# Identity products in TensorE's waits, and expert weights read from HBM tile by tile, in a perceiver layer with a mixture of experts

## What is computed

```
x = x + cross_attention(context, context, layernorm(x))      # 16 heads of 8
x = x + latent_attention(layernorm(x))                       # 8 heads, compressed keys and values
x = x + experts(layernorm(x))

def experts(x):                                              # 8 experts, 2 for each row, I = 352
    logits = x @ w_router.T;  probs = softmax(logits)
    topw, topi = top_k(probs, 2);  topw = topw / sum(topw)
    gate = silu(einsum('th,eih->eti', x, w_gate))
    up   = einsum('th,eih->eti', x, w_up)
    down = einsum('eti,ehi->eth', gate * up, w_down)
    out  = einsum('eth,te->th', down, combine)               # combine holds topw at topi
```

## Time and profile before

| | us |
|---|---|
| three timed runs | 517.17, 521.39, 521.87 |
| their median | 521.39 |
| the profiled execution | 524.1 |
| its span, first to last instruction | 522.0 |
| TensorE busy, matmuls (3931 of them) | 418.8 |
| VectorE busy | 333.3 |
| ScalarE busy | 312.3 |
| GpSimd busy | 206.2 |

### The profile page before, as it was taken

The page is one execution under the profiler, slowest core; times in us unless marked ns, Lnnn a source line. Parts: engine busy times, 40 slices in busy tenths (PEclk is TensorE's granted clock), DMA queues, the critical chain, the costliest instruction groups (busy, mean ns, idle before and its releaser), DMA issues.

```text
span 522.0 us, 13730 instructions
## 1 busy us (share of the span) xinstructions
PE 418.8 (80%) x3931; PEld 339.0 (65%) x3931; DVE 333.3 (64%) x990; ACT 312.3 (60%) x914; POOL 206.2 (40%) x482
## 2 busy tenths in 40 slices
PE   0997999999999999999758898883578686868850
PEld 0565677777777777777537787772478686767850
DVE  4477688888888888888654878675433333333325
ACT  3586788888888888888666776220233333333333
POOL 0545355555555555554200000000336555556630
PEclk9999899999999999999978999875589897999985
DMA  6268111111111111110000000010011111111107
GB/s 166 60 219 334 32 40 40 32 38 40 40 30 40 40 40 31 40 40 0 2 1 0 2 2 0 1 64 17 16 30 42 42 42 35 42 41 43 40 31 242
DMA packets 21054, 26.63 MB, mean 51 GB/s; under 512 B 4736, under 2 KB 17984, under 8 KB 20512
## 3 DMA queue, kind: packets, MB, share of 16 engines
q1 hardware_dynamic: 18528, 21.13, 12.9%
q0 software_dynamic: 2496, 5.12, 3.3%
HBM read 21.59 MB, written 4.65 MB: 50 GB/s over the span
## 4 chain that ended last, share of the span: by engine, by line
PE 30%; another core or an unknown queue 6%; DVE 5%; ACT 5%; issue 3%; DMA 2%; ACTq 0%; POOL 0%; POOLq 0%; DVEq 0%; SPq 0%
PE PS L1074 10%; PE PS L944 4%; PE PS L974 3%; PE PS L1082 3%; PE PS L1066 2%; PE PS L1004 2%; PE PS L957 1%; PE PS L990 1%; PE PS L1038 1%; PE PS L1059 1%; PE PS L981 1%; ACT GC L525 1%; ACT SE L464 1%; ACT XGT L513 1%
## 5 line engine op out<-in xcount | busy, mean ns | idle before, releaser
L389 ACT ACTIVATE PR<-PS,nmax 128x257 f32<-128x257 f32 x256 | 117.9, 474 | 30.9 <-DVE nmax L586 30.4
L586 DVE TENSOR_REDUCE nmax<-PS 128x1 f32<-128x257 f32 x256 | 90.6, 416 | 25.7 <-PE PS L868 25.4
L875 PE MATMUL PS<-I,PR 128*128 128x128 f32 x512 | 66.4, 273 | 0.0
L339 POOL DMA_INDIRECT XG<-x_table,IDX x39 | 38.0, 975 | 61.9 <-DVE IDX L786 50.3
L1074 PE MATMUL PS<-XGT,GC 128*128 128x128 f32 x234 | 39.2, 309 | 28.4 <-ACT XGT L513 25.8
L875 PEld LDWEIGHTS PS<-I,PR 128*128 128x128 f32 x512 | 57.9, 141 | 0.3 <-issue 0.3
L350 POOL DMA_INDIRECT y_table<-YS,IDY x39 | 38.5, 986 | 45.3 <-DVE YS L797 39.2
L293 POOL TENSOR_TENSOR O<-OM 128x64 f32<-128x64 f32 x64 | 20.4, 319 | 88.2 <-DVE OM L609 88.2
L792 DVE TENSOR_TENSOR H<-PS,SG 128x384 f32<-128x384 f32 x39 | 21.7, 557 | 52.0 <-issue 20.0
L1074 PEld LDWEIGHTS PS<-XGT,GC 128*128 128x128 f32 x234 | 32.9, 212 | 33.2 <-ACT XGT L513 29.5
L389 ACT ACTIVATION_READ_ACCUMULATOR PR<-PS,nmax 128x1 f32 x256 | 52.0, 203 | 0.0
(11 more groups left out here) (191 smaller groups left out, 849.3 us busy)
## 6 DMA issues: line engine op xcount, KB each, us to landing
CR<-ctxT SPq DMA_DIRECT2D x64, 128.0 KB, 2.1
Y<-y_table SPq DMA_DIRECT2D x4, 512.0 KB, 4.9
GW<-w_gate SPq DMA_DIRECT2D x1, 1536.0 KB, 6.9
UW<-w_up SPq DMA_DIRECT2D x1, 1536.0 KB, 10.1
DW<-w_down SPq DMA_DIRECT2D x1, 1536.0 KB, 12.6
NAMES<-lanes SPq DMA_DIRECT2D x1, 1344.0 KB, 16.6
X<-x SPq DMA_DIRECT2D x4, 256.0 KB, 3.6
x_table<-xe SPq DMA_DIRECT2D x4, 256.0 KB, 2.4
```

The costliest lines, as they stand in the source:

```text
L389: a.activation(PR[:, j % 2, gr, 0:S], src, ACT.Exp, bias=bias, accum_out=rsum[:, j % 2, gr:gr + 1]).then_inc(exped, 1)
L586: v.tensor_reduce(nmax[:, gr:gr + 1], bank[gr][:, 0:S], AX.X, ALU.max, negate=True).then_inc(max_ready, 1)
L875: ins = t.transpose(bank[4 + ch][:, 128 * gr:128 * gr + 128], PR[:, j % 2, gr, KC * ch:KC * ch + KC], I128[:, :])
```

## The change

TensorE computes products of the identity with itself, whose results nobody reads, at eight places (6, 5, 3, 2, 3, 10, 12 and 12 products in the order of the code's run: `keep_busy`). The gate and up weights are no longer loaded whole. SP reads the owners from `offset`, and loads for each tile the owner's 384 columns of both weights from HBM straight into `GC` and `UC`, which are now rings of four. The copies of ScalarE and VectorE go, and so do their reads of the owners. The down weights stay as they are.

```
-        GW = sb("GW", [128, E * IP])
-        UW = sb("UW", [128, E * IP])
-        GC, UC = sb("GC", [128, 2, IP]), sb("UC", [128, 2, IP])
+        GC, UC = sb("GC", [128, WRING, IP]), sb("UC", [128, WRING, IP])      # WRING = 4
+        gate_in, up_in = ([sem(f"{w}_in{n}") for n in range(WRING)] for w in ("gate", "up"))
 sync:
-            sp.dma_start(GW[:, :], w_gate).then_inc(in_moe, 16)
-            sp.dma_start(UW[:, :], w_up).then_inc(in_moe, 16)
...
+            own = []                                    # behind the stores of x_table
+            sp.wait_ge(c["step"], owner_steps)
+            for s in range(TILES):
+                if s % 4 == 0:
+                    owners_of(mybir.EngineType.SP, own, s)
+                if s >= WRING:
+                    sp.wait_ge(c["gate"], s - WRING + 1)
+                sp.dma_start(GC[:, s % WRING, :], w_gate[:, bass.ds(own[s], IP)]).then_inc(gate_in[s % WRING], 16)
+                if s >= WRING:
+                    sp.wait_ge(c["up"], s - WRING + 1)
+                sp.dma_start(UC[:, s % WRING, :], w_up[:, bass.ds(own[s], IP)]).then_inc(up_in[s % WRING], 16)
 scalar:
-            def gate_weights(s):
-                if s % 4 == 0:
-                    owners_of(mybir.EngineType.Activation, own, s)
-                if s >= 2:
-                    a.wait_ge(c["gate"], s - 1)
-                a.activation(GC[:, s % 2, :], GW[:, bass.ds(own[s], IP)], ACT.Copy).then_inc(c["gate_w"], 1)
 vector:
-            def up_weights(s):
-                if s % 4 == 0:
-                    owners_of(mybir.EngineType.DVE, own, s)
-                if s >= 2:
-                    v.wait_ge(c["up"], s - 1)
-                v.tensor_copy(UC[:, s % 2, :], UW[:, bass.ds(own[s], IP)]).then_inc(c["up_w"], 1)
 tensor:
+            def keep_busy(n, bk):
+                for m in range(n):
+                    t.matmul(bank[bk][:, 0:128], I128[:, :], I128[:, :], start=True, stop=True)
             for n in range(-2, PAIRS + 1):
+                if n == -1:
+                    keep_busy(6, 4)                     # ahead of queries_and_keys(1)
+                if n == PAIRS - 1:
+                    keep_busy(3, 1)                     # ahead of turn_probs(6)
...
+                if n == PAIRS - 1:
+                    keep_busy(2, 1)                     # ahead of weigh_compressed(6)
...
+                if n == -1:
+                    keep_busy(5, 5)                     # ahead of turn_queries(0, 1)
                 if n == PAIRS:
                     for m in range(3):
                         turn_rows_of(m)
+                    keep_busy(3, 0)                     # ahead of latent_out(7)
...
             route(3)
+            keep_busy(10, 0)
...
             t.matmul(bank[5][:, 0:128], TOT[:, :], parts["tile_earlier"], start=False, stop=True).then_inc(c["placed"], 1)
+            keep_busy(12, 0)                            # ahead of the 32 matmuls of L1059
...
-                for name, w, bk in (("gate", GC, s % 2), ("up", UC, 2 + s % 2)):
-                    t.wait_ge(c[name + "_w"], s + 1)
+                for name, w, bk, in_w in (("gate", GC, s % 2, gate_in), ("up", UC, 2 + s % 2, up_in)):
+                    t.wait_ge(in_w[s % WRING], 16 * (s // WRING) + 16)
...
+            keep_busy(12, 0)                            # ahead of turn_rows(0)
```

More of the change, by code:

```diff
@@ L26 @@
 TILES = (2 * B * L + E * 127) // 128
-XRING, YRING = 4, 4
+XRING, YRING, WRING = 4, 4, 4
 EPS = 1e-5
@@ L177, in build @@
             "owners", "chosen", "named", "valued", "rowed", "listed", "silu_set", "ids", "second", "w_out", "x_stored", "xg_turned", "xg_copied",
-            "gate_w", "up_w", "gate", "up", "silu", "hidden", "down", "ys", "summed", "out")}
+            "gate", "up", "silu", "hidden", "down", "ys", "summed", "out")}
         gathered = [sem(f"gathered{n}") for n in range(XRING)]
         scattered = [sem(f"scattered{n}") for n in range(YRING)]
+        gate_in, up_in = ([sem(f"{w}_in{n}") for n in range(WRING)] for w in ("gate", "up"))
         in_y = [sem(f"in_y{n}") for n in range(4)]
@@ L502, in _ @@
             copied(3)
-            a.wait_ge(in_moe, 16 * 6)
+            a.wait_ge(in_moe, 16 * 4)
             a.wait_ge(c["totals"], 1)
@@ L518, in gated @@
                 a.activation(SG[:, s % 2, :], bank[s % 2][:, 0:IP], ACT.Silu).then_inc(c["silu"], 1)
-            own = []
-            def gate_weights(s):
-                if s % 4 == 0:
-                    owners_of(mybir.EngineType.Activation, own, s)
-                if s >= 2:
-                    a.wait_ge(c["gate"], s - 1)
-                a.activation(GC[:, s % 2, :], GW[:, bass.ds(own[s], IP)], ACT.Copy).then_inc(c["gate_w"], 1)
-            a.wait_ge(c["step"], owner_steps)
-            gate_weights(0)
             turned_rows(0)
             for s in range(TILES):
-                if s + 1 < TILES:
-                    gate_weights(s + 1)
                 gated(s)
@@ L797, in scaled @@
                 v.tensor_copy(YS[:, s % YRING, :], bank[4 + s % 2][:, 0:D]).then_inc(c["ys"], 1)
-            own = []
-            def up_weights(s):
-                if s % 4 == 0:
-                    owners_of(mybir.EngineType.DVE, own, s)
-                if s >= 2:
-                    v.wait_ge(c["up"], s - 1)
-                v.tensor_copy(UC[:, s % 2, :], UW[:, bass.ds(own[s], IP)]).then_inc(c["up_w"], 1)
-            up_weights(0)
             for s in range(TILES):
-                if s + 1 < TILES:
-                    up_weights(s + 1)
                 multiplied(s)
@@ L1039, in route @@
                 ins.then_inc(c["logits"], 1)
-            t.wait_ge(in_moe, 16 * 6)
+            t.wait_ge(in_moe, 16 * 4)
             for n in range(3):
@@ L1073, in gate_and_up @@
                     for n in range(IC):
-                        ins = t.matmul(bank[bk][:, 128 * n:128 * n + 128], w[:, s % 2, 128 * n:128 * n + 128], XGT[:, s % 2, :],
+                        ins = t.matmul(bank[bk][:, 128 * n:128 * n + 128], w[:, s % WRING, 128 * n:128 * n + 128], XGT[:, s % 2, :],
                                        start=True, stop=True)
```

## The result

Before 522.16 us (median of 16 runs, 517.17 to 525.08), after 516.06 us (16 runs, 512.96 to 518.14): ratio 0.9884, with a 95% interval of 0.9858 to 0.9909, 6.1 us less. I had forecast 507.4. The direction and the range (481 to 519) hold, and the median lies at the very end of the forecast's own range, 499 to 516; of the 14.0 us that I had summed up, 6 came. (The median of three runs that I had started from, 521.39, was itself 0.8 us low.)

A forecast was written before the change was run, and what follows sets the result against it. Bounds: one late context block, low TensorE clock after idle times, a tile loop with late TensorE signals tied to POOL's transfers. Terms sum to -14.0: 524.1 to 510.1 us profiled, less 2.7, 507.4 median; own range 499 to 516, 8 in 10 481 to 519.

The forecast's parts named there:

- (1): Attention over the context: without the two whole loads, block 8 lands earlier, its wait and low clock go; -5.7 us.
- (2): Latent pipeline filling: six and five products fit in idle time and keep the clock up; -4.4 us.
- (3): Last latent pairs: three and two products, and three ahead of latent_out(7), hide in waits and save low clock; -2.1 us.
- (4): Routing: ten and twelve products bring the clock up so the list's matmuls end earlier, six chances in ten; -1.4 us.
- (5): Ahead of turn_rows(0): twelve products give the first tiles the high clock, six chances in ten; -1.7 us.
- (6): Tile loop: removing ScalarE's and VectorE's copies gains nothing, as they are not in POOL's cycle; 0, at best -4.1 us.
- (7): Tile loop: 78 weight transfers of 192 KB on SP cost the gathers some time; +1.3 us, ends 0 and +35.
- Rival A: Tile loop: the copies held back POOL and TensorE's signals, so 25 us go, 482 us; chance 0.14.
- rival B: Tile loop: weights get ahead of the gathers, each 0.9 us later, 35 us slower, 542 us; chance 0.08.
- C: All product places: the products don't hold the clock and the last three batches overrun, 518.5 us; chance 0.10.
- D: Context attention: the early wait stays or is made up elsewhere, 513.1 us; chance 0.08.

The follow-up runs named there:

- e2: Kernel before with the identity products alone, loads and copies as before; ratio 0.9917 to the kernel before.
- e11: Kernel before with VectorE doing YS of the last tile ahead of H of this one, nothing else; 517.84 us, ratio 0.998.
- e3: Kernel before with the two whole weight loads issued behind the last context block; ratio 0.9925 to the kernel before.
- e4: Kernel before with the products and the whole loads issued late, copies kept, no weight transfers per tile; 511.57 us, ratio 0.9806.
- e10: e4 with VectorE doing YS of the last tile ahead of H of this one; 505.96 us, ratio 0.9721.
- e12: e7 with 22 products in place of 12 at two places, ahead of the list and of the first turned tile; 507.48 us, ratio 0.9779.
- e1: Kernel after without its identity products; ratio 1.0002 to the kernel before.
- e6: Kernel after with each weight transfer issued a second time into spare rings, TensorE waiting for both; 514.54 us, ratio 0.986.
- e7: Kernel after with VectorE doing YS of the last tile ahead of H of this one; 509.23 us, ratio 0.9758.

## Why the prediction went wrong where it did

*(1) The whole loads: -5.7 forecast, -3.9 (plus or minus 1.6) measured.* The mechanism holds. At context block 8 the kernel after gains 5.4 us on the one before, and it keeps that to 243 us. Then 1.1 come back: the clock falls at 249 (between 248.6 and 251.1) in every profile of the table whose loads are out of the way, and in none of the three that have them early (before, e2, e11). "nothing else is late in it, so this should reach the end" is the sentence that failed: the wait was taken away with its low stretch, and another low stretch came 200 us later. Why it comes there the runs don't show. Without the products the latent attention takes 86 us in place of 83.6 or 81.5 besides (clock 0.57 from 322.4 to 346.3 in e3); the products mend that.

*(2) and (3) The products in the latent attention: -6.5 forecast.* To the first xe the profiles have 83.6, 86.1, 85.9 and 81.5 us without products, 84.3 in the mean, and 77.4 or about 79.1 with them, 78.3 over the eight: -6.0. The places and the costs of the products are as worked out. The terms were read from one execution, though, and e11 shows another, of the same code there, that has no low stretch at the last pairs: 2.1 us less without any product.

*(4) and (5) Routing and first tiles: -3.1 forecast.* Kernels with copies take 42.6 us here without products (before, e3, e11) and 39.4 with them (e2, e4, e10): -3.1. The parts are others than forecast. The term "at the high clock the 32 matmuls of L1059 are bound by VectorE's comparisons" was wrong: e12 shows them at that clock, and they take as long. What came instead is that TensorE reached the first tiles at the high clock in all eight profiles with products, to within 0.2 us, where I had given six chances in ten.

So the products give 9.1 us up to the first scatter by the profiles, for 9.6 forecast, and 4.3 to 6.2 in the timed comparisons. This is the largest part of the miss, 3.4 us, and its size fits with which executions were profiled. Over the whole span the three pairs of profiles have 9.6 (before and e2), 6.3 (e3 and e4) and 11.5 us (e1 and after), where the timed runs have 4.3, 6.2 and 6.2. The profiled executions of before, e1 and e3 took 1.9, 3.9 and 1.9 us more than the medians of their kernels; those of e2, e4 and after -2.1, +1.1 and -1.3. That makes the products look 3.3 us better in the profiles than in the timed runs. So the step that failed is the pricing: the sum took every low stretch of one execution that was slow for its kernel as if each execution had it. It then took off another 2.7 us to get from that execution to the median, and if the stretches made it slow, this counts them twice; how much of it, the runs don't show. What sets the time of a timed run isn't its clock alone, either: in the 16 runs of the kernel after, clock (0.932 to 0.962) and time don't go together, and the longest run has the highest clock.

*(6) and (7) Copies and transfers: +1.3 forecast, +4.1 measured (+4.0, plus or minus 2.3, without products).* No run takes the copies away without putting the transfers there, so what each of the two terms is worth alone isn't shown. Rival A's 25 us didn't come: its sign was under 115 us from the first turned tile, and it is 131.4. The first gather lost 1.0 us and not 0.3 in after, 1.3 in e6 and 1.7 in e1, and the stage to the first scatter 1.6 (41.0 to 41.2, for 39.4). The loop has the rest: 123.5 us in the mean of e1, e6 and after, 120.9 in that of before, e2, e3 and e4, though single profiles of one loop lie 3 us and more apart. "What they can cost is the gathers' time" is the step that failed here. It isn't the DMA engines' time, from which I had priced the transfers: e6 doubles that and isn't slower, and rival B falls with it. What the term left out is VectorE's turn at the end of a pause: H ahead of YS keeps a waiting scatter 0.46 us longer, and without the copies VectorE came to be in that order more often. The count above makes it 2.3 of the 2.6 us, and e7, which takes the order away, gets back 6.6. That is in favour of this cause and does not prove it: why the first gather takes longer is open, and e10 is still 1.9 us (plus or minus 5.4) below e7. The working has a small slip besides: 20 x 0.28 x 0.2 is 1.1, not 1.0.

*The rivals.* C would have been 518.5, and D 513.1. C's mechanism is refuted by the clock in the latent attention, and D's holds in part: a fifth of (1) was made up elsewhere. That 516.06 lies beside C's number is chance.

*The sum.* -5.7, -9.6 and +1.3 were -3.9, -6.2 and +4.1: three terms that were all too hopeful, by 1.8, 3.4 and 2.8 us.

## What to carry to other kernels

Read low-clock stretches from several executions before each is priced: they wander from one to the next, and when one goes another can come later. Where a loop is held by a late signal and not by an engine, bandwidth and busy time don't price it; look at what the waiting engine does first when the signal comes, and put first what the bottleneck waits for. Split a joint change: here one part (no copies, weights from HBM) ate two thirds of what the products brought, and swapping two lines was worth about as much as the whole (6.6 us, plus or minus 3.7).

## What the runs showed of the hardware

TensorE's signals reach ScalarE and VectorE 2.8 us and more behind the end of its rows while POOL issues gathers and scatters back to back (53.3 us of waits on H alone, the longest 4.0; 27 of 30 such waits end 0.90 to 1.03 us behind the end of a transfer of POOL), and with only one kind of them the loop is 81.7 us in place of 121.7. With a stream of transfers that keeps the DMA engines busy to 0.83 (e6), a 128-row gather still takes POOL 0.97 us, and the kernel is 1.3 us faster, plus or minus 3.7, than with half the stream. The bfloat16 weight loads of SA, each 128x128 and read with a stride, take 144 ns in the mean at either clock level (e12).
